# Three setup blocks merged into one, relation sums and projection merged into 25 turns

## The reference

```python
edge_index = jnp.stack([src, dst])
h = jnp.maximum(_layernorm(x, axis=-1), 0.0)
x = x + L0(h)      # gated sum: segment_sum of h[src] W_msg + embed[type9], then a GRU cell
h = jnp.maximum(_layernorm(x, axis=-1), 0.0)
x = x + L1(h)      # normalized graph convolution, its own layer norm
h = jnp.maximum(_layernorm(x, axis=-1), 0.0)
x = x + L2(h)      # relations: 50 types as mixtures of 4 bases, summed by src
h = jnp.maximum(_layernorm(x, axis=-1), 0.0)
x = x + L3(h)      # edge softmax over dst with 4 heads, output projection, layer norm
```

## Time and profile before

| what | us |
|---|---|
| median of 3 runs (9898.41 to 9905.25) | 9899.51 |
| the profiled execution | 9904.95 |
| its span | 9903.2 |
| index setup | 0 to 101 |
| first norm | 101 to 238 |
| weights | 238 to 266.5 |
| L0 sums and GRU | 266.5 to 2376.5 |
| L1 sums | 2376.5 to 4446 |
| L2 relation messages | 4446 to 7370.5 |
| relation sums, norm, projection | 7370.5 to 7819.5 |
| L3 softmax and output | 7819.5 to 9903 |

### The profile page before, as it was taken

The page is one execution under the profiler, slowest core; times in us unless marked ns, Lnnn a source line. Parts: engine busy times, 40 slices in busy tenths (PEclk is TensorE's granted clock), DMA queues, the critical chain, the costliest instruction groups (busy, mean ns, idle before and its releaser), DMA issues. The chain is left out here.

```text
span 9903.2 us, 151998 instructions
## 1 busy us (share of the span) xinstructions
PE 7208.4 (73%) x34582; PEld 5568.9 (56%) x34582; DVE 4971.3 (50%) x12398; ACT 1950.4 (20%) x5096; POOL 7033.3 (71%) x6298
## 2 busy tenths in 40 slices
PE   0466566665777777769889888888850389999998
PEld 0355555554444444437777777777740267777776
DVE  3444444445677777762222222222224267777776
ACT  1011111111122222222222222222210112222221
POOL 0677777776777777767888888888860277777775
PEclk6555555555555555557777777777765555555555
DMA  3422222222333333334444444444444233333332
GB/s 115 162 66 66 66 66 66 66 66 63 82 87 87 87 87 87 87 94 55 55 56 55 56 55 56 55 56 55 56 71 136 69 89 91 91 93 91 92 91 68
DMA packets 836506, 766.48 MB, mean 77 GB/s; under 512 B 142123, under 2 KB 728537, under 8 KB 836296
## 3 DMA queue, kind: packets, MB, share of 16 engines
q0 software_dynamic: 376576, 415.18, 24.5%
q1 hardware_dynamic: 396808, 298.65, 9.9%
q10 hardware_dynamic: 62912, 50.63, 1.6%
HBM read 538.59 MB, written 225.30 MB: 77 GB/s over the span
## 5 line engine op out<-in xcount | busy, mean ns | idle before, releaser
L1449 POOL DMA_INDIRECT scat<-msg_out,msg_idx x1568 | 2418.8, 1543 | 492.3 <-issue 346.3
L2028 POOL DMA_INDIRECT soft_rows<-proj,soft_slot x1568 | 1497.2, 955 | 962.7 <-ACT soft_slot L2049 494.3
L734 POOL DMA_INDIRECT L_rows<-H,L_slot x1568 | 1568.1, 1000 | 762.8 <-issue 477.0
L998 POOL DMA_INDIRECT L_rows<-H,L_slot x1568 | 1534.0, 978 | 497.0 <-issue 477.3
L1541 PE MATMUL msg_ps_msg<-msg_hb,msg_lhs 128*128 128x128 f32 x6272 | 1601.0, 437 | 1.6 <-DVE msg_lhs L1514 1.6
L1541 PEld LDWEIGHTS msg_ps_msg<-msg_hb,msg_lhs 128*128 128x128 f32 x6272 | 1493.1, 328 | 188.2 <-issue 185.9
L1514 DVE SCALAR_TENSOR_TENSOR msg_lhs<-msg_dst_sp,msg_node,msg_ps_c 128x512 f32<-128x512 f32 x784 | 551.2, 745 | 2034.7 <-ACT msg_dst_sp L1469 2029.6
L873 PE MATMUL L_sum<-L_onehot,L_rows 128*128 128x64 f32 x3136 | 703.2, 399 | 799.8 <-DMA L_rows<-H,L_slot 786.7
L873 PEld LDWEIGHTS L_sum<-L_onehot,L_rows 128*128 128x128 f32 x3136 | 644.0, 304 | 889.4 <-DVE L_hi_hot L807 401.5
L1203 PE MATMUL L_sum<-L_onehot,L_rows 128*128 128x64 f32 x3136 | 761.6, 425 | 470.0 <-DMA L_rows<-H,L_slot 435.6
L1203 PEld LDWEIGHTS L_sum<-L_onehot,L_rows 128*128 128x128 f32 x3136 | 698.0, 327 | 663.4 <-issue 440.6
(11 more groups left out here) (361 smaller groups left out, 10323.5 us busy)
## 6 DMA issues: line engine op xcount, KB each, us to landing
L_rows<-H,L_slot POOLq DMA_INDIRECT x3136, 2.5
msg_hb<-HB SPq DMA_DIRECT2D x392, 128.0 KB
soft_at_in<-in_edge_attr_dram SPq DMA_DIRECT2D x391, 128.0 KB
scat<-L_zeros SPq DMA_DIRECT2D x64, 408.0 KB, 5.4
rel_parts<-scat SPq DMA_DIRECT2D x200, 128.0 KB, 2.7
HB<-L_prod ACTq DMA_DIRECT2D x49, 512.0 KB, 3.0
scat<-msg_out,msg_idx POOLq DMA_INDIRECT x1568, 3.3
soft_rows<-proj,soft_slot POOLq DMA_INDIRECT x1568
```

The lines of the kernel that those rows point to most:

```text
L734: pool.indirect_dma_start(rows[:, k, j, :], None, t["H0"], bass.IndirectOffsetOnAxis(ap=slot[:, k, j:j + 1], axis=0)).then_inc(gathered[k] ...
L998: pool.indirect_dma_start(rows[:, k, j, :], None, t["H1"], bass.IndirectOffsetOnAxis(ap=slot[:, k, j:j + 1], axis=0)).then_inc(gathered[k] ...
L1449: pool.indirect_dma_start(t["scat"][j], bass.IndirectOffsetOnAxis(ap=idx[:, k, j:j + 1], axis=0), out[:, k, j, :], None, compute_op=ALU.ad ...
L2028: pool.indirect_dma_start(rows[:, s % SC, j, :], None, t["proj"], bass.IndirectOffsetOnAxis(ap=slot[:, s, j:j + 1], axis=0)).then_inc(gath ...
```

## The change

It has three parts.

**One setup block.** Index setup, first norm and weight work stand in one block. ScalarE's queue loads x in four chunks, stores X0 in four chunks, and norms in place; SyncE's queue has the index loads, the weight loads, four chunks of H0 and then the index rows. GpSimd fills only the last 512 columns of the index tiles. VectorE has statistics (written out, 98 times), constants, index work and weight work in this order. Several index tiles share memory.

```diff
+        @block.scalar
+        def _(act):
+            for q in range(CHUNKS):
+                act.dma_start(xs[:, cuts[q]:cuts[q + 1], :], x[cuts[q] * P:cuts[q + 1] * P, :].rearrange("(n p) f -> p n f", p=P)).then_inc(x_in[q], 16)
...
+            for q in range(CHUNKS):
+                act.wait_ge(x_in[q], 16 + 16 * (q == CHUNKS - 1 and rest_n > 0))
...
+                act.dma_start(t["X0"].rearrange("(n p) f -> p n f", p=P)[:, ends[q]:ends[q + 1], :], xs[:, ends[q]:ends[q + 1], :]).then_inc(x_out[q], 16)
+            act.wait_ge(n0_step, 1 + NT + 7)
+            act.activation(var[:, :], var[:, :], ACT.Sqrt).then_inc(n0_step, 1)
...
+            for q in range(CHUNKS):
+                sp.wait_ge(normed, max(0, min(ends[q + 1], NT)))
+                sp.dma_start(t["H0"].rearrange("(n p) f -> p n f", p=P)[:, ends[q]:ends[q + 1], :], xs[:, ends[q]:ends[q + 1], :]).then_inc(h_out, 16)
...
         setup_phase(nc, S, a, t)
-        first_norm_phase(nc, S, a["x"], t)
-        weights_phase(nc, S, a, t)
```

```diff
         @block.tensor
         def _(pe):
+            pe.sem_inc(multiplied, R)
             pe.wait_ge(counts, 3)
             pe.matmul(ps_hist[:, 0:HI], none[:, :], none[:, 0:HI], start=True, stop=False, skip_group_check=True)
-            pe.sem_inc(multiplied, R)
...
-            v.memset(acc, 0.0).then_inc(added, 1)
             v.memset(zeros[:, :, :], 0.0).then_inc(degrees, 1)
             v.memset(t["dinv_src"][:, :], 0.0).then_inc(degrees, 1)
             v.tensor_scalar(deg[:, :], t["deg_src"][:, :], 1.0, None, ALU.max).then_inc(degrees, 1)
+            v.memset(acc, 0.0).then_inc(added, 1)
...
             def before():
+                v.sem_inc(x_made, B)
```

```diff
+            def sum_copies(i):
+                k, link = i % DEPTH, Link(v, dv, 1 + i * E)
+                v.wait_ge(loaded[k], (i // DEPTH + 1) * (16 * COPIES + 16))
+                link(v.tensor_tensor(parts[:, k, 0:HALF, :], parts[:, k, 0:HALF, :], parts[:, k, HALF:COPIES, :], ALU.add))
+                link(v.tensor_tensor(total[:, :, :].rearrange("p n f -> p (n f)"), parts[:, k, 0, :], parts[:, k, 1, :], ALU.add))
+                if i >= 2:
+                    v.wait_ge(stored[i % 2], landed(i))
...
+            for i in range(TURNS):
+                sum_copies(i)
+                if i:
+                    add_bias(i - 1)
+                else:
+                    v.sem_inc(dv, Q // 2)
+                scale(i)
...
+            for i in range(TURNS):
+                act.wait_ge(dv, 1 + i * E + C)
+                act.activation(var[:, :], var[:, :], ACT.Sqrt).then_inc(acted, 1)
+                if i:
+                    store_products(i - 1)
+                    act.wait_ge(pe_done, i * 2 - 1)
+                act.wait_ge(dv, 1 + i * E + E)
+                for q in range(Q):
+                    act.activation(h_q[:, q, :], res[:, i % 2, q, :], ACT.Relu, bias=mean[:, q:q + 1], scale=var[:, q:q + 1]).then_inc(acted, 1)
+                act.wait_ge(pe_done, i * 2 + 1)
+                act.activation(hT[:, i % 2, :], ps_h[:, :], ACT.Copy).then_inc(acted, 1)
+                act.dma_start(tiles_of(t["X3"], i * Q, Q), res[:, i % 2, :, :]).then_inc(stored[i % 2], 16)
+                act.wait_ge(acted, i * CA + CA)
+                act.dma_start(t["H3T"][:, i * (Q * P):(i + 1) * (Q * P)], hT[:, i % 2, :]).then_inc(stored[i % 2], 16)
```

More of the change, by code:

```diff
@@ new lines, in setup_phase @@
+        ps_head = c.enter_context(nc.psum_tensor("w_ps_head", [P, 512], F32))
+        w_loaded, w_turned, w_taken, w_step, w_by_head = (sem(f"w_{n}") for n in ("loaded", "turned", "taken", "step", "by_head_made"))
+        block = c.enter_context(nc.Block())
+        row = lambda ap, n=P: ap.rearrange("(a f) -> a f", a=1).broadcast_to([n, ap.shape[0]])
+        loads = [(nat[:, m, :], a[w][q * P:(q + 1) * P, 0:F]) for m, (w, q, _, _) in enumerate(square)]
+        loads += [(edge_nat[:, h, :], a["L3_gnn_W_proj_w"][:, F:F + ED]) for h in range(2)]
@@ L129, in setup_phase @@
+        for j in range(J):
+            own = slice(DEN * j, DEN * j + T9)
+            loads += [(msg_b[own, :], row(a["L0_gnn_b_msg"], T9)), (t["embed_b"][own, :], a["L0_gnn_edge_embed"])]
         parts = [(b, min(P, full - b * P)) for b in range(NB) if full > b * P]
@@ L188, in _ @@
         def _(v):
+            v.memset(xs[:, full_n:TR, :], 0.0).then_inc(n0_step, 1)
+            v.memset(msg_b[:, :], 0.0).then_inc(w_step, 1)
+            v.memset(t["embed_b"][:, :], 0.0).then_inc(w_step, 1)
+            for i in range(NT):
+                for q in range(CHUNKS):
+                    if i == ends[q]:
+                        v.wait_ge(x_in[q], 16 + 16 * (q == CHUNKS - 1 and rest_n > 0))
+                v.bn_stats(stats[:, i:i + 1, :], xs[:, i:i + 1, :]).then_inc(n0_step, 1)
+            link = Link(v, n0_step, 1)
+            link.n = NT
+            v.wait_ge(n0_step, 1 + NT)
+            norm_constants(link, v, stats, mean, var, tmp)
+            v.wait_ge(n0_step, 1 + NT + 8)
+            link.n += 1
+            link(v.reciprocal(var[:, :], var[:, :]))
+            link(v.scalar_tensor_tensor(mean[:, :], mean[:, :], -1.0, var[:, :], ALU.mult, ALU.mult), False)
             link = Link(v, step)
@@ L1253, in _ @@
         def _(sp):
-            sp.wait_ge(taken, 1)
-            for q in range(extra // P):
-                sp.dma_start(tiles_of(table, S.NTP + q, 1), pads[:, :, :]).then_inc(saved, 16)
-            sp.sem_inc(free, 1)
-            with sp.Fori(0, TURNS) as i:
-                sp.wait_ge(out, i * 2 + 4)
-                sp.dma_start(tiles_of(table, i * Q, Q), prod[:, :, :]).then_inc(saved, 16)
-                if h_table is not None:
-                    sp.wait_ge(taken, i + 2)
-                    sp.dma_start(h_table[:, ds(i * (Q * P), Q * P)], hT[:, :]).then_inc(saved, 16)
-                sp.wait_ge(saved, i * (16 * stores) + 16 * stores + 16 * (extra // P))
-                sp.sem_inc(free, 1)
+            for i in range(TURNS):
+                k = i % DEPTH
+                if i >= DEPTH:
+                    sp.wait_ge(dv, 1 + (i - DEPTH) * E + 2 + Q)
+                for q in range(COPIES):
+                    sp.dma_start(parts[:, k, q, :].rearrange("p (n f) -> p n f", n=Q), tiles_of(t["scat"][q], i * Q, Q)).then_inc(loaded[k], 16)
+                sp.dma_start(x_q[:, k, :, :], tiles_of(t["X2"], i * Q, Q)).then_inc(loaded[k], 16)
@@ L1269, in _, with store_products @@
         @block.scalar
         def _(act):
[L1271 to L1282 removed]
+            def store_products(i):
+                act.wait_ge(dv, 1 + (i + 1) * E + C + Q // 2 if i < TURNS - 1 else 1 + TURNS * E + Q // 2)
+                act.dma_start(tiles_of(t["proj"], i * Q, Q), prod[:, i % 2, :, :]).then_inc(stored[i % 2], 16)
@@ L1284, in _ @@
+            store_products(TURNS - 1)
+            for k in range(2):
+                act.wait_ge(stored[k], 48 * len(range(k, TURNS, 2)) + 16 * extra * (k == 0))
         @block.tensor
         def _(pe):
[L1286 to L1297 removed]
@@ L1299, in _ @@
-        @block.vector
-        def _(v):
-            v.memset(pads[:, :, :], 0.0).then_inc(taken, 1)
-            v.sem_inc(out, 2)
-            with v.Fori(0, TURNS) as i:
-                v.wait_ge(turned, i + 2)
-                v.wait_ge(free, i + 1)
-                v.tensor_copy(hT[:, :], ps_h[:, :]).then_inc(taken, 1)
-                v.wait_ge(based, i + 1)
-                if bias is None:
-                    for k in range(Q // 2):
-                        cp = v.tensor_copy(prod[:, k, :], ps_b[:, k, 0:WD])
-                    cp.then_inc(out, 1)
-                else:
-                    v.tensor_tensor(prod[:, 0:2, :], ps_b[:, 0:2, 0:WD], bcast(bias[:, :], 1, 2), ALU.add).then_inc(out, 1)
-                    v.tensor_tensor(prod[:, 2:4, :], ps_b[:, 2:4, 0:WD], bcast(bias[:, :], 1, 2), ALU.add).then_inc(out, 1)
```

428 lines of the change are left out of this document (167 added, 261 removed).

## The result

The changed kernel takes 9528.64 us (median of 4 runs, 9524.82 to 9531.87), the kernel before on the same chip 9900.35 us: a ratio of 0.9624, 95% interval 0.9607 to 0.964. The sign is right; 371.7 us are saved where 452.9 were forecast, and the time lies 14 us above the range. The profiled execution has a span of 9530.1 us, 373.1 less than before, so the two traces can be laid side by side.

The account below looks back on a forecast made before the run. GpSimd, gathering back to back, was taken to bound four phases, so only first-gather starts and the stretches without GpSimd work counted. Savings 141.7 + 69.7 + 241.5 = 452.9 from 9899.5 gave 9447 us; forecast 9430 to 9475 (0.52), range 9405 to 9515.

Parts of the forecast that it names:

- Part 1: Setup: three blocks become one, with index work and weights ending at 124.8 instead of 266.5 us; 141.7 us saved.
- 31 + 16.5 - 3 = 44.6: First block: time in us when ScalarE can issue the fourth X0 store, once the third is nearly taken.
- Part 2: Heads of both sum phases and the softmax phase: first gathers start earlier by 26.7, 15.0 and 28.0, together 69.7 us.
- they stay saved: Gather phases: the 69.7 us of earlier starts last, because GpSimd is the bound and consumers catch up.
- short casts: Head of the second sum phase: by the skill's rule, the only instructions that could hold a gather up.
- Part 3: Relation sums, norm and projection become 25 pipelined turns of 7.6 us: 207.6 instead of 449.1 us, 241.5 saved.
- turn = 4.1 + L: Relation turns: VectorE's 4.1 us after the products' landing plus landing time L, taken as 3.5 us, gives 7.6 us.
- standing behind a whole turn of loads: Relation turns: a store waits for 4.4 us of loads, landing 7.1 us, turn 11.2; 9530 us, chance 0.04.
- Rival 2: Relation turns: stores land late under the loads, turns of 9.5 us, 44 us worse, 9491 us; chance 0.20.
- rival 3: Heads of gather phases: gathers don't proceed beside the memset, so the earlier starts are worth nothing; 9517 us, chance 0.08.
- rival 5: Whole kernel: fetching some 1600 straight-code instructions at 0.35 us each loses 560 us, slower than before, 10007 us; chance 0.02.
- Rival 1: Relation turns hide the store wait (6.8 us) and X0 stores don't block: 18 + 6 us better, 9423 us; chance 0.15.

Follow-up runs that it names:

- the delayed loads: Changed kernel, still two buffers, with SyncE issuing the relation block's next loads at the turn's end, behind the products' issue: 10977.7 us on the slower chip, ratio 0.9615.
- the third buffer: Changed kernel with three instead of two buffers for summed rows, transposed rows and products in the relation block: 9472.22 us, ratio 0.9574.
- the two edits around the cast: Changed kernel with L1's large cast waiting for the memset's end and a 98-element cast put behind L0's memset: 10998.62 us on the slower chip, ratio 0.9629.
- the relation block alone: Kernel before with only the 25-turn block of relation sums, norm and projection: 9703.01 us, ratio 0.9815; on the slower chip 11217.7 us, ratio 0.982.
- the three cures: Changed kernel with third relation buffer, square root ahead of X0 stores, and L1's cast waiting for the memset: 9443.91 us, ratio 0.9541; slower chip 10932.66 us, 0.9573.

## Why the prediction was wrong

**The bound** was read rightly. On the usual chips GpSimd never rests in the gather phases, and the head starts cost or gained nothing through empty rings.

**Part 1**, 13 of 82 us. The step that failed is "31 + 16.5 - 3 = 44.6" for the fourth X0 store (it adds up to 44.5). The index work started at 61.8 us, past the 60 us that the prediction had named as a sign of being wrong. The step let the DMA engines be free of loads at 32 us and gave X0 their whole width, 22 us. SyncE's queue carried 3.64 MB beside it, so ScalarE's second, third and fourth issues took 11.2, 8.7 and 9.4 us in place of some 5.5. All other terms of the part were right to about 2 us. That the issue blocks ScalarE at all was the right mechanism; its cure, the root ahead of the stores, gave back 17 us, the 13 and 4 more.

**Part 2**, 9 us of L1. The first gathers came 2.0 us later, 1.7 earlier and 0.2 earlier than forecast. That L0 gave 27.9 us where 26.7 were forecast is luck: 24.6 stood at the first gather, and the rest lies within what L0 varies by. The sentence that failed is "they stay saved". The rival, a memset that keeps GpSimd from working, named the wrong instruction: beside the memset the gathers of L0 run freely. It was the cast queued behind it. The prediction's sentence on the Trainium skill (SBUF — State Buffer, Who interferes with whom, the practical consequences) allowed only "short casts" to hold a gather up. The traces agree with the page on which instruction does it (a cast, not a memset) and with its rule that a VectorE instruction with two SBUF inputs contends with a GpSimd instruction that reads SBUF: gathers beside the second scan take up to 1.83 us. Its inference, in the same place, that `tensor_tensor` doesn't stall the generating of descriptors is not borne out for these gathers: beside the comparison of L0 they take up to 1.47 us. No sentence there has a cast holding a gather while it is still queued, for 13.07 and 23.62 us.

The 12.5 us of the softmax phase belong to the same sentence. I took gathers as costing the same wherever they fall, and passed over that rule on two SBUF inputs. A gather that starts inside a long enough VectorE instruction with two SBUF operands is longer, and either half of the change moved the pattern.

**Part 3**, 47 us. The mechanism was right in each point: turn = 4.1 + L, the wait ahead of the scaling, released by the products. The term that was mis-sized is L, 3.5 us taken, 5.7 measured: 21 turns at 9.81 in place of 7.6 are 46.4 us; a later first root costs 2.5 and a longer end 1.3, a shorter first turn returns 0.8 and the two turns without loads 1.8. The earlier trace rows had both ends, 2.7 and 5.4, and I went toward the free one "because the stores' own queue is short". What counts is what is under way on the DMA engines when the store is issued, on whatever queue; two issues by ScalarE in one turn, 2.7 and 5.7 us, show it, and the delayed loads (products 3.6 us, X3 4.8) prove it. The Trainium skill (DMA: Bandwidth & Descriptors, queues, rings and completion order) has each engine take turns between queues by packets. The measured landing lies between sharing as I drew it (3.5) and standing behind a whole turn of loads (7.1), because the loads have a start of 2.6 us: the products land about when the last of them does. Taking turns alone was no ground for the lower value.

**The rivals.** Rival 2 (turns of 9.5, 9491 us) happened in full, with a chance of 0.20. The other 37 us up to 9528 come from two places that had no rival with a price, the X0 stores sharing with SyncE's loads and gathers beside VectorE's two-operand work, and from rival 3 in part and by another instruction. Straight code (rival 5) cost nothing that shows: 98 statistics in 0.2 us each and 7.01 us turns with the third buffer. Rival 1 is what the kernel becomes when both waits are cured, though it took edits: with the wait ahead of the cast besides, 9443.91 us against its 9423.

## What to carry to other kernels

Size a wait on a store by the landing under the traffic that is issued ahead of it, on all queues, and give a double-buffered store that is issued late in a turn a third buffer or let the loads go out behind it. When several terms are each a wait that others' traffic can lengthen, their misses tend to one sign, as here in all four places; widen the range to that side. When GpSimd is the bound, look at what VectorE runs and has queued beside it: put a wait between a long memset and a large cast behind it, and where it can be had, keep one operand of VectorE's two-operand work in PSUM.

## What the runs showed of the hardware

- A cast of 1568 elements queued without a wait behind a memset held a gather for 13.06 to 13.13 us (seven traces, at least four chips, memset of 10.94 us) and 23.62 us (one trace, memset of 21.82 us); with a wait between them the gather took 0.95 us, and the one that met the cast itself 1.29 to 1.32 us (four traces). A cast of 98 elements held none, and took 0.35 us itself.
- A gather that starts while VectorE runs an instruction with two SBUF operands ends no sooner than 0.76 us (scan of 32x512) or 0.82 us (tensor_tensor) behind it; one that started ahead of the scan isn't held (none of some 400 in twelve traces). Beside reductions, memsets and instructions with a PSUM operand a gather takes 0.94 to 0.96 us.
- A store of 264 KB landed in 2.5 to 2.9 us free, 3.6 us when issued 0.3 us ahead of 1.28 MB of loads on another queue, 5.7 us when issued 2.6 us behind the first of them, about when the last of them landed. A store of 256 KB took 2.7 and 4.8 us in the same two kernels, the other way round.
- On one chip the kernel before took 11418 us and not 9896. The message phase took 2895 us on both, but L0, L1 and the softmax phase took 2342, 2426 and 2705 us in place of 2041, 2021 and 1987 (the changed kernel with the two edits around the cast, and the changed kernel): there GpSimd waited again and again for free places in the ring, 454 us in L1 alone, so that the consumers and no longer GpSimd set the pace. What slowed them is open. The ratios of the same kernels stayed close (0.982 and 0.9815 for the relation block alone, 0.9573 and 0.9541 for the three cures).
